# Two pipelined attention runs: a reordered head, with the first stack's issues dealt to two queues by halves

## Chip, cores and metric

The kernel runs on one core of one Trainium2 chip. The metric is the device time of one execution, in microseconds (us), the median of three runs.

## What is computed

The reference is a chain of four transformer layers on x of shape 8 x 256 x 128 (batch, tokens, features). Each has a modulation from a condition vector c, an attention and a feed-forward part:

```python
mod = (_silu(c) @ wmod).reshape(8, 6, 1, -1)          # sa, ca, ga, sb, cb, gb
ga = (2 * (ga >= 0) - 1) * jnp.maximum(jnp.abs(ga), 0.25)   # gb in the same way
h = _layernorm(x) * (1 + ca) + sa
x = x + ga * attention(h)
h = _layernorm(x) * (1 + cb) + sb
x = x + gb * feed_forward(h)
```

The change touches layer 0 (its attention with ALiBi slopes, and its feed-forward part, which is itself a rotary attention followed by a mixture of four experts) and the attention of layer 2. All three are causal, with 16 heads of 8 features. Shift, scale and gate of the feed-forward part are sb, cb and gb.

## The kernel before

**Runs and passes.** One pass m handles one batch of 256 tokens. The first pipelined run holds passes 0 to 15 (0 to 7 are the attention of layer 0, 8 to 15 its feed-forward part), the second one passes 16 to 23 (attention of layer 2). Each engine has its own program, in an order written out by hand; they meet only in semaphores. `pass_done` at the end of a phase opens the next one.

**Stacks.** Queries and keys (128 x 512 float32) are split into three bfloat16 parts each by GpSimd (`split_qk`, five instructions, lines 776 to 780). Small DMAs then copy them into a stack of rows that one matmul takes in full precision: `expand_half(queue, m, u)` issues 12 of them (6 for each side i of the partitions, which are partitions 0 to 63 and 64 to 127) for the half u of the heads, 24 a stack. There are three stacks, used in turn. Except for the first stack of a run, the Sync queue issues all 24. In pass 0 and in pass 16 Sync issues half u=0 and ScalarE's queue half u=1. The stack of pass m+1 can only be built after `parts_split(m)`; that of pass m+3 only once the turned scores of pass m have been computed, and the split of pass m+2 overwrites the parts of pass m, so that it waits until the stack of pass m has landed.

**Iterations.** The iteration for pass m (line `for m, there in iterations(ph)`) goes through six units k. In each, TensorE computes the turned scores of pass m (lines 1100 to 1108) and the scores of pass m+1 (lines 1074 to 1082, into the banks called `scored`), VectorE reduces the latter to maxima (`max_piped`, line 2169), and ScalarE takes the exponential of the former (`exp_piped`, line 3180). The iteration before pass `first` has the scores of the first pass alone. GpSimd splits the maxima (`split_max`, lines 762 to 766), TensorE turns them, and ScalarE puts them into the stack with two DMAs (`place_max`, line 3191); the turned scores need them.

**The head of a run.** Ahead of the iterations lie three fronts (passes first, first+1 and first+2). Each is: normalise (VectorE, `norm_piped`, line 2126), statistics of the pass two further on (`stats_piped`), turn (TensorE, line 1166), features (ScalarE, `take_normed`, line 3208), projections (TensorE, lines 1173 and 1177), intake (VectorE, lines 2176 and 2177), split (GpSimd). Each engine takes these in the order of its program. In between lie:

- on ScalarE, the issue of half u=1 of the first stack, behind the features of the first pass and ahead of those of the second
- in the first run, clearing three stacks by copies from a staging area: stacks 0 and 2 by VectorE (lines 2238 and 2241), stack 1 by ScalarE (line 3249); Sync and ScalarE wait for all of them (`stacks_clear`) before they issue
- on VectorE, behind all three fronts, `gates_piped` of the attention (four instructions, lines 2139 to 2144, that read `scored`), and in the first run `mod_ffn`: shift and scale of the feed-forward part (lines 2150 and 2151), its gates (the same four lines again, from `scored` again) and six small instructions (lines 2154 to 2159)
- on TensorE, behind the three fronts of the first run, the matmuls for these (`spread_mod`, line 1039): two groups at once and the third when `scored` has been read
- on GpSimd, behind the three fronts, `prepare_piped` (four clears, line 789, each with two settings of small areas)

The first scores of the first run wait for `mod_taken` 6, which is the end of all of VectorE's `mod_ffn`; those of the second run wait for the attention's gates.

## Time and profile before

| | |
|---|---|
| median of three runs | 2599.92 us (2599.36 to 2601.29) |
| the profiled execution, its own time | 2596.48 us |
| its span in the trace | 2594.7 us |
| mean granted TensorE clock | 0.767 |
| first run: first front to first reduction of scores | 9.5 to 57.7 us |
| second run: last x of the phase before to first reduction of scores | 1762.4 to 1805.2 us |

The trace is of one execution, so its span is what a sum of its rows explains; 1.8 us lie around it. The two heads are stretches of some 45 us each in which every engine is mostly idle. An engine name with a q (SPq, ACTq) is that engine's instruction queue issuing DMAs. Times within the trace count from the start of the span. Clock 1.00 is TensorE's upper level (2.4 GHz), 0.50 its lower one (1.2 GHz).

### The profile page before, as it was taken

To read this page: it belongs to the slowest core of one execution; us is meant where nothing else is said; L and a number is where in the kernel's file an instruction comes from. 1 tells how busy PE (TensorE), PEld (TensorE's weight loads), DVE (VectorE), ACT (ScalarE), POOL (GpSimd) and SP (SyncE) were. 2 spreads that over 40 slices of the span, in tenths; PEclk is the share of its full clock that TensorE was granted. 3 is DMA by queue.
4 is the path that set the end of the run, shared out by engine and by line. 5 is a ranking of instruction groups with operands and counts; after the bars stand their busy time and mean duration, and the time that the engine had idled before them with its cause. 6 is when DMAs were issued, how large, how long until landed. Compare 5 with 4: busy or idle time off the path is not lost.

```text
span 2594.7 us, 44049 instructions
## 1 busy us (share of the span) xinstructions
PE 1990.5 (77%) x14690; PEld 1394.5 (54%) x14690; DVE 1673.0 (64%) x5279; ACT 1148.5 (44%) x3370; POOL 894.2 (34%) x1171
## 2 busy tenths in 40 slices
PE   3878888874377667665687999994875799999945
PEld 2545666661265556554584666662543466667632
DVE  5787443335778887888847666664755466666547
ACT  1443333427677677767411222220442255565610
POOL 3433121014457655764540000003410155555512
PEclk7987889875555555555558999995995799999967
DMA  3111001010000000000010000001111000000000
GB/s 116 43 42 42 19 15 35 2 78 23 13 13 7 11 9 14 7 7 1 1 46 1 1 0 0 0 0 39 48 33 62 11 1 1 1 1 1 1 1 17
DMA packets 57809, 49.61 MB, mean 19 GB/s; under 512 B 7048, under 2 KB 55912, under 8 KB 57064
## 3 DMA queue, kind: packets, MB, share of 16 engines
q1 hardware_dynamic: 54548, 45.53, 5.5%
q10 hardware_dynamic: 3040, 1.38, 0.3%
q8 instruction: 108, 1.77, 0.3%
q14 instruction: 113, 0.93, 0.1%
HBM read 19.78 MB, written 1.05 MB: 8 GB/s over the span
## 4 chain that ended last, share of the span: by engine, by line
PE 44%; DVE 28%; ACT 8%; issue 7%; SPq 5%; POOL 5%; ACTq 1%; DMA 0%; DVEq 0%; POOLq 0%
PE bank L1544 5%; PE bank L1536 5%; PE bank L1537 5%; SPq L566 4%; DVE weights L2524 4%; PE bank L1613 3%; PE bank L1266 3%; ACT rope_c L3334 3%; ACT rope_s L3334 3%; PE bank L1282 3%; PE bank L1650 3%; PE bank L1662 2%; DVE small L2562 2%; DVE feat_o L2574 2%; POOL big L717 1%
## 5 line engine op out<-in xcount | busy, mean ns | idle before, releaser
L1450 PE MATMUL bank<-V,probsT 128*128 128x9 f32 x1024 | 234.7, 362 | 79.5 <-ACT probsT L3345 79.5
L1450 PEld LDWEIGHTS bank<-V,probsT 128*128 128x128 f32 x1024 | 224.9, 327 | 116.5 <-ACT probsT L3345 97.3
L2169 DVE TENSOR_REDUCE nmax<-bank 128x4 f32<-128x1024 f32 x144 | 176.1, 1223 | 81.3 <-PE bank L1082 81.2
L3400 ACT ACTIVATE hid<-bank 128x512 f32<-128x512 f32 x144 | 85.7, 597 | 283.3 <-PE bank L1537 272.0
L1544 PEld LDWEIGHTS bank<-weights,hid 128*128 128x128 f32 x1152 | 151.0, 192 | 78.9 <-issue 75.6
L2758 DVE TENSOR_TENSOR hid<-hid,bank 128x512 f32<-128x512 f32 x144 | 98.7, 688 | 127.3 <-PE bank L1544 123.2
L1544 PE MATMUL bank<-weights,hid 128*128 128x128 f32 x1152 | 152.5, 276 | 12.7 <-DVE hid L2758 10.3
L3345 ACT ACTIVATE probsT<-bank 128x512 f32<-128x512 f32 x128 | 76.0, 597 | 179.7 <-PE bank L1437 177.3
L1536 PE MATMUL bank<-O,weights 128*128 128x512 f32 x288 | 150.2, 604 | 2.7 <-DVE big L2698 2.7
L1537 PE MATMUL bank<-O,weights 128*128 128x512 f32 x288 | 148.3, 597 | 0.0
L804 POOL MEMSET big<- 128x4096 bf16 x1 | 3.5, 3511 | 411.7 <-DVE x L2796 411.7
L2772 DVE SCALAR_TENSOR_TENSOR O<-bank,O 128x128 f32<-128x128 f32 x496 | 138.9, 343 | 0.0
L2943 DVE TENSOR_TENSOR kT<-bank,weights 128x256 f32<-128x256 f32 x128 | 54.1, 423 | 123.3 <-PE bank L1613 123.1
L717 POOL TENSOR_TENSOR big<-big,rinv 128x512 f32<-128x512 f32 x128 | 131.7, 1050 | 4.0 <-DVE rinv L2936 4.0
L3434 ACT ACTIVATE big<-bank,nmax 128x256 f32<-128x256 f32 x256 | 118.7, 473 | 16.7 <-DVE nmax L2931 16.7
L3180 ACT ACTIVATE feat_o<-bank 128x1024 f32<-128x1024 f32 x72 | 73.7, 1024 | 117.5 <-PE bank L1108 87.9
L3180 ACT ACTIVATE O<-bank 128x1024 f32<-128x1024 f32 x72 | 73.8, 1024 | 110.2 <-PE bank L1108 82.4
L2451 DVE TENSOR_REDUCE nmax<-bank 128x2 f32<-128x512 f32 x128 | 84.9, 683 | 34.1 <-PE bank L1424 34.1
L1424 PE MATMUL bank<-qT 48*128 48x256 bf16 x256 | 70.3, 402 | 45.7 <-ACT weights L3288 33.3
L2931 DVE TENSOR_REDUCE nmax<-bank 128x2 f32<-128x512 f32 x128 | 82.3, 684 | 30.6 <-PE bank L1624 30.6
L725 POOL TENSOR_TENSOR kT<-kT 128x256 f32<-128x256 f32 x64 | 46.8, 731 | 137.4 <-DVE kT L2944 137.4
L1537 PEld LDWEIGHTS bank<-O,weights 128*128 128x128 f32 x288 | 55.5, 193 | 70.5 <-issue 70.5
(652 smaller groups left out, 5531.5 us busy)
## 6 DMA issues: line engine op xcount, KB each, us to landing
qT<-parts SPq DMA_DIRECT2D x276, 32.0 KB
big<-V SPq DMA_DIRECT2D x192, 32.0 KB
big<-parts SPq DMA_DIRECT2D x180, 32.0 KB
weights<-in_weights_l_ffn SPq DMA_DIRECT2D x1, 4832.0 KB, 15.0
weights<-in_weights_l_attn SPq DMA_DIRECT2D x1, 3904.0 KB, 12.7
weights<-in_weights_l_ffn SPq DMA_DIRECT2D x1, 3628.0 KB, 13.9
qT<-V SPq DMA_DIRECT2D x96, 32.0 KB
weights<-in_weights_l_ffn SPq DMA_DIRECT2D x1, 2304.0 KB, 7.8
```

The costliest lines, as they stand in the source:

```text
L566: queue.dma_start(stacks[m % STACKS][to, u * HALF:(u + 1) * HALF], pair_of(m, at, *of)).then_inc(stack_in[u].sem, 16)
L717: nc.gpsimd.tensor_tensor(row, row, rinv[:, h % H, :].unsqueeze(2).to_broadcast([P, T, S]), ALU.mult).then_inc(scaled.sem, 1)
L1450: last = mm(pb[1][:, t * S + h * wide:t * S + (h + 1) * wide], probsT[:, h % 2, at:at + P], values_of(b, k)[:, h * wide:(h + 1) * wide], s ...
L1536: mm(pb[two][:], W(ph, "gate")[:, cols], pair_feat, start=True, stop=True)
L1537: mm(pb[two + 1][:], W(ph, "up")[:, cols], pair_feat, start=True, stop=True).then_inc(hid_psum.sem, 1)
L1544: last = mm(pb[6 + e % 2][:, j * D:(j + 1) * D], risen(e)[:, j * P:(j + 1) * P], W(ph, "down")[:, e * D:(e + 1) * D], start=True, stop=True)
L2169: V_.tensor_reduce(to, scored.rearrange("p (i a n) -> p i a n", i=HPG, n=n), AX.X, ALU.max, negate=True).then_inc(score_max.sem, 1)
L2524: link(V_.tensor_scalar(at_most[:, j, :], row_of(b, j), tried[at][:, 0, j:j + 1], 0.0, ALU.is_le, ALU.add, accum_out=tried[at][:, 1, j:j + ...
L2772: last = V_.scalar_tensor_tensor(pair_sum[:, j, :], down[:, j, :], w, pair_sum[:, j, :], ALU.mult, ALU.add)
L3180: nc.scalar.activation(turned_probs[n % TURNS], turned_scores, ACT.Exp).then_inc(turned_exp.sem, 1)
L3334: nc.scalar.activation(signs[signed[0] % len(signs)], row_of(b, j), ACT.Sign, bias=tried[at][:, 0, j:j + 1], scale=-1.0, accum_out=tried[a ...
L3434: last = nc.scalar.activation(probs3[h % SLOTS3][:, t * S:(t + 1) * S], pb[h % 3][:, t * S:(t + 1) * S], ACT.Exp, bias=nmax[:, h % H, t:t ...
```

## The change

In ScalarE's program the features of the second pass now come ahead of its first issues, and those of the third pass in the middle of them. The first stack is dealt out by sides instead of by head halves: Sync issues side 0 of both halves, ScalarE side 1 of both, 12 DMAs each as before. In the first run ScalarE clears stacks 1 and 2, VectorE stack 0 alone. VectorE computes the attention's gates ahead of the intake of the second pass. TensorE computes the scale of the feed-forward part ahead of the third front, into `scored`, and VectorE takes it there ahead of the third intake; the feed-forward gates go through banks 4 and 5 (`raw`). The first scores wait for `mod_taken` 3 (mod, gates, scale), the first turned scores for 6.

```diff
@@ -557,9 +557,9 @@
             return 0 <= n < N3
-        def expand_half(queue, m, u):
-            for i in range(HPG):
+        def expand_half(queue, m, u, sides=range(HPG)):
+            for i in sides:
                 for slot, of in enumerate(SLOTS):
                     to = slice(64 * i + HD * slot, 64 * i + HD * slot + HD)
                     at = slice((2 * i + u) * HD * HALF, (2 * i + u + 1) * HD * HALF)
@@ -663,14 +663,14 @@
                         for i in range(HPG):
                             at = 64 * i + STACK_ROWS
                             sp.dma_start(stacks[m % STACKS][at:at + ALI_ROWS, :, 0, :], no_bias).then_inc(bias_gone, 16)
-                    for u in range(2 if m > first else 1):
+                    for u in range(2):
                         if m > first:
                             sp.wait_ge(stack_in[u].sem, stack_in[u](m, 0))
                         if m >= first + STACKS:
                             sp.wait_ge(turned_psum.sem, turned_psum(m - STACKS, 3 * u + 3))
-                        expand_half(sp, m, u)
+                        expand_half(sp, m, u, range(HPG) if m > first else (0,))
             load(1)
             for i, ph in enumerate(WEIGHED):
@@ -1039,13 +1039,16 @@
                     last = mm(to[:, b * D:(b + 1) * D], silu_n[:, b, :], W(ph, "wmod")[:, j * D:(j + 1) * D], start=True, stop=True)
                 last.then_inc(mod_psum, 1)
+            def scale_of_ffn(ph="l0_ffn"):
+                pe.wait_ge(loaded[1], 16)
+                pe.wait_ge(mod_taken, 2)
+                spread_mod(ph, 1, scored)
             def mod_ffn(ph="l0_ffn"):
-                pe.wait_ge(loaded[1], 16)
                 spread_mod(ph, 0, turned_scores)
-                spread_mod(ph, 1, ps[:, 4:6, :].rearrange("p c n -> p (c n)"))
-                pe.wait_ge(mod_taken, 2)
-                spread_mod(ph, 2, scored)
+                spread_mod(ph, 2, ps[:, 4:6, :].rearrange("p c n -> p (c n)"))
                 nc.tensor.transpose(pb[7][:, 0:P], W(ph, "n1"), C("ident"))
                 nc.tensor.transpose(pb[7][:, P:2 * P], W(ph, "n2"), C("ident"))
                 nc.tensor.transpose(pb[7][0:64, 2 * P:3 * P], W(ph, "lng"), C("ident"))
@@ -1055,7 +1058,7 @@
                 kind, u, h0 = UNITS[k]
                 if k == 0 and place_of(m) == 0:
-                    pe.wait_ge(mod_taken, 6 if m == 0 else MODS["l2_attn"] + 2)
+                    pe.wait_ge(mod_taken, 3 if m == 0 else MODS["l2_attn"] + 2)
                 if k == 0 and B <= m < B + STACKS:
                     pe.wait_ge(bias_gone, 16 * HPG * (m - B + 1))
@@ -1085,6 +1088,9 @@
             def turned_scores_piped(m, k):
                 kind, u, h0 = UNITS[k]
+                if k == 0 and m == 0:
+                    pe.wait_ge(mod_taken, 6)
                 if k % 3 == 0:
                     pe.wait_ge(nmax_in[u].sem, nmax_in[u](m + 1, 0))
@@ -1287,6 +1293,8 @@
                 first = RUNS[ph][0]
                 mod_piped(ph)
                 for m in fronts(ph):
+                    if m == 2:
+                        scale_of_ffn()
                     turn_normed(m)
                     project_qk(m)
                 if ph == "l0_attn":
@@ -2133,23 +2141,27 @@
                 link(V_.tensor_copy(shift_n, pb[6][:, 0:B]))
                 V_.tensor_scalar(scale_n, pb[6][:, B:2 * B], 1.0, None, ALU.add).then_inc(mod_taken, 1)
-            def gates_piped(to, n_psum, n_taken):
+            def gates_piped(to, n_psum, n_taken, raw):
                 dve.wait_ge(mod_psum, n_psum)
-                link(V_.tensor_scalar(mag_n, scored, -1.0, 0.25, ALU.mult, ALU.max))
-                link(V_.tensor_scalar(two_n, scored, 0.0, 2.0, ALU.is_ge, ALU.mult))
-                linkup()
-                link(V_.tensor_tensor(mag_n, scored, mag_n, ALU.max))
+                link(V_.tensor_scalar(mag_n, raw, -1.0, 0.25, ALU.mult, ALU.max))
+                link(V_.tensor_scalar(two_n, raw, 0.0, 2.0, ALU.is_ge, ALU.mult))
+                linkup()
+                link(V_.tensor_tensor(mag_n, raw, mag_n, ALU.max))
                 linkup()
                 V_.scalar_tensor_tensor(to, two_n, 1.0, mag_n, ALU.subtract, ALU.mult).then_inc(mod_taken, 1)
                 dve.wait_ge(mod_taken, n_taken)
+            def scale_of_ffn():
+                dve.wait_ge(mod_psum, 3)
+                V_.tensor_scalar(scale_ffn, scored, 1.0, None, ALU.add).then_inc(mod_taken, 1)
             def mod_ffn():
                 dve.wait_ge(mod_psum, 4)
                 V_.tensor_copy(shift_ffn, turned_scores).then_inc(mod_taken, 1)
-                V_.tensor_scalar(scale_ffn, ps[:, 4:6, :].rearrange("p c n -> p (c n)"), 1.0, None, ALU.add).then_inc(mod_taken, 1)
-                gates_piped(gates_ffn, 5, 5)
+                gates_piped(gates_ffn, 5, 5, ps[:, 4:6, :].rearrange("p c n -> p (c n)"))
                 dve.wait_ge(mod_psum, 6)
                 link(V_.tensor_copy(norm1_n, pb[7][:, 0:1]))
                 link(V_.tensor_copy(norm2_n, pb[7][:, P:P + 1]))
@@ -2230,16 +2242,21 @@
                 stats_piped(first)
                 mod_piped(ph)
                 stats_piped(first + 1)
-                for m in fronts(ph):
-                    norm_piped(m)
-                    stats_piped(m + 2)
-                    if m == 0:
-                        dve.wait_ge(ali_loaded, 16 * HPG * 2)
-                        V_.tensor_copy(stacks[0].rearrange("p g side n -> p (g side n)"), staging).then_inc(stacks_clear, 1)
-                    intake_piped(m)
-                    if m == 0:
-                        V_.tensor_copy(stacks[2].rearrange("p g side n -> p (g side n)"), staging).then_inc(stacks_clear, 1)
-                gates_piped(gates_attn, MODS[ph] + 2, MODS[ph] + 2)
+                norm_piped(first)
+                stats_piped(first + 2)
+                if ph == "l0_attn":
+                    dve.wait_ge(ali_loaded, 16 * HPG * 2)
+                    V_.tensor_copy(stacks[0].rearrange("p g side n -> p (g side n)"), staging).then_inc(stacks_clear, 1)
+                intake_piped(first)
+                norm_piped(first + 1)
+                stats_piped(first + 3)
+                gates_piped(gates_attn, MODS[ph] + 2, MODS[ph] + 2, scored)
+                intake_piped(first + 1)
+                norm_piped(first + 2)
+                stats_piped(first + 4)
+                if ph == "l0_attn":
+                    scale_of_ffn()
+                intake_piped(first + 2)
                 if ph == "l0_attn":
                     mod_ffn()
                 for m, there in iterations(ph):
@@ -3241,17 +3258,20 @@
             def piped(ph):
                 first = RUNS[ph][0]
-                for m in fronts(ph):
-                    take_normed(m)
-                    if m == first:
-                        if ph == "l0_attn":
-                            act.wait_ge(ali_loaded, 16 * HPG * 2)
-                            nc.scalar.activation(stacks[1].rearrange("p g side n -> p (g side n)"), staging, ACT.Copy).then_inc(stacks_clear, 1)
-                            act.wait_ge(stacks_clear, 4)
-                        else:
-                            act.wait_ge(ali_loaded, 16 * HPG * (2 + STACKS))
-                        act.wait_ge(parts_split.sem, parts_split(m, 1))
-                        expand_half(act, m, 1)
+                take_normed(first)
+                if ph == "l0_attn":
+                    act.wait_ge(ali_loaded, 16 * HPG * 2)
+                    for st in stacks[1:]:
+                        nc.scalar.activation(st.rearrange("p g side n -> p (g side n)"), staging, ACT.Copy).then_inc(stacks_clear, 1)
+                take_normed(first + 1)
+                if ph == "l0_attn":
+                    act.wait_ge(stacks_clear, 4)
+                else:
+                    act.wait_ge(ali_loaded, 16 * HPG * (2 + STACKS))
+                act.wait_ge(parts_split.sem, parts_split(first, 1))
+                expand_half(act, first, 0, (1,))
+                take_normed(first + 2)
+                expand_half(act, first, 1, (1,))
                 for m, there in iterations(ph):
                     for k in range(NU):
                         if m >= first and k == 2 and there(3):
```

## Rows read from the trace of the kernel before

**Rows 1.** Chain that ended last, from 1750 to 1970 us, its shares by line.
```profile
by line: SPq L566 52.7%; issue 9.3%; ACTq L566 3.9%; DVE big L1892 1.9%; PE bank L1544 1.7%; PE bank L1039 1.7%; DMA big<-V 1.4%; ACT O L3180 1.4%; DVE big L1873 1.4%; POOL big L979 1.3%; PE bank L1536 1.2%; PE bank L1537 1.2%; PE bank L117
```

**Rows 2.** Timeline, first head: start, length, engine, line, what, [idle before <- releaser].
```profile
11.14 3.78 PE L1039 MATMUL bank<-weights,feat_o 128*128 128x128 f32 x16
...
15.85 3.60 ACT L3249 ACTIVATE big<-big 128x4096 bf16<-128x4096 f32 x1
...
17.97 2.29 DVE L2241 CAST big<-big 128x4096 bf16<-128x4096 f32 x1
...
18.12 2.60 POOL L776 CAST parts<-weights 128x512 bf16<-128x512 f32 x1 [5.04 <-DVE weights L2177]
...
24.62 8.80 SPq L566 DMA_DIRECT2D qT<-parts  x12
24.62 9.79 ACTq L566 DMA_DIRECT2D qT<-parts  x12
...
34.46 0.56 ACT L3208 ACTIVATE V<-bank,small 128x256 f32<-128x256 f32 x1 [15.01 <-issue]
...
38.13 0.66 POOL L776 CAST V<-weights 128x512 bf16<-128x512 f32 x1 [12.84 <-DVE weights L2177]
...
39.65 0.56 ACT L3208 ACTIVATE V<-bank,small 128x256 f32<-128x256 f32 x1 [4.62 <-PE bank L1166]
```

**Rows 3.** Timeline, first head: modulation of the feed-forward part, first reduction.
```profile
42.14 4.24 PE L1039 MATMUL bank<-weights,feat_o 128*128 128x128 f32 x32
...
43.57 1.22 DVE L2139 TENSOR_SCALAR feat_o<-bank 128x1024 f32<-128x1024 f32 x1
...
48.62 2.55 PE L1039 MATMUL bank<-weights,feat_o 128*128 128x128 f32 x16 [2.24 <-DVE weights L2144]
...
57.69 1.23 DVE L2169 TENSOR_REDUCE nmax<-bank 128x4 f32<-128x1024 f32 x1 [1.08 <-PE bank L1082]
```

**Rows 4.** Timeline of the Sync queue: issues of whole stacks (24) or half ones (12).
```profile
42.63 17.64 SPq L566 DMA_DIRECT2D big<-V  x24
60.38 18.37 SPq L566 DMA_DIRECT2D big<-parts  x24
...
84.99 17.93 SPq L566 DMA_DIRECT2D qT<-V  x24
...
1781.02 8.78 SPq L566 DMA_DIRECT2D big<-parts  x12
...
1798.24 17.43 SPq L566 DMA_DIRECT2D big<-V  x24
...
1905.59 18.33 SPq L566 DMA_DIRECT2D big<-V  x24
```

**Rows 5.** Timeline, second head and the first iterations behind it.
```profile
1778.05 0.34 DVE L2012 TENSOR_SCALAR small<-small 128x2 f32<-128x2 f32 x1
...
1790.07 0.56 ACT L3208 ACTIVATE V<-bank,small 128x256 f32<-128x256 f32 x1 [16.71 <-issue]
...
1804.63 0.52 POOL L789 MEMSET big<- 128x512 f32 x1
...
1805.24 1.23 DVE L2169 TENSOR_REDUCE nmax<-bank 128x4 f32<-128x1024 f32 x1 [1.15 <-PE bank L1082]
...
1811.35 0.20 POOL L762 CAST small<-nmax 128x16 bf16<-128x16 f32 x1 [4.02 <-DVE nmax L2169]
...
1819.65 1.02 ACT L3180 ACTIVATE feat_o<-bank 128x1024 f32<-128x1024 f32 x1 [3.17 <-PE bank L1108]
...
1832.14 0.61 POOL L780 CAST V<-weights 128x512 bf16<-128x512 f32 x1
```

**Rows 6.** Stretches: bounds, length, busy time of each engine, granted clock, DMA share, GB/s.
```profile
22.00:26.00 4.00, 0.69 (x2) 0.29 (x2) 1.77 (x7) 0.00 (x0) 3.06 (x4) 0.50 0.00 0
...
314.00:330.00 16.00, 16.00 (x99) 13.69 (x98) 2.81 (x12) 5.38 (x14) 0.00 (x0) 1.00 0.01 3
```

**Rows 7.** Chain that ended last in order of time: landing of the last stack.
```profile
1922.38 3.19 DMA big<-V
```

## Prediction, made before the change was run

> **What bounds the kernel now.** I read the stretches and the chain that ended last first, since busy shares say nothing of two short heads. In the second run, that chain goes through the Sync queue for more than half of the stretch around it [rows 1]: behind the first stack, which the two queues issue by halves, six stacks lie between the issue at 1798.24 and the last one at 1905.59, 107.35 us or 17.9 us a stack, where 24 issues of 0.73 us take 17.5 [rows 4]. Sync goes from one stack into the next without a rest. So this run ends as many us earlier as the stack of its second pass is begun earlier, unless another engine then falls behind. In the first run the queue has one rest: the stack of pass 2 is issued by 60.38 + 18.37 = 78.75, that of pass 3 starts at 84.99 [rows 4]. It waits for the split of pass 3, which hangs on the iterations; these hang on the first reduction of scores at 57.69 [rows 3]. The rest is 6.2 us.
>
> What holds both heads up is plain in the timeline. ScalarE issues 12 DMAs from 24.62 to 34.41 and only then takes the features of pass 1 at 34.46 [rows 2]; in the second run that row is 1790.07 [rows 5]. VectorE, TensorE and GpSimd stand still meanwhile.
>
> **First run: Sync queue.** ScalarE now clears two stacks: 15.85 + 3.60 + 3.60 = 23.05 [rows 2]. The split of pass 0 takes 4.50 us where nothing is in its way (start of pass 1's split 38.13, issue behind it 42.63) [rows 2, 4]; its first instruction took 2.60 us instead of 0.66 beside VectorE's copy of 17.97, which goes away [rows 2]. So it ends at 22.6, and the issues start at 23.05 instead of 24.62. Sync's 12 take 8.80 and end at 31.9.
>
> The Trainium skill (SBUF — State Buffer, section Who interferes with whom) says that VectorE in a two-port mode and GpSimd lock each other out for a whole instruction. The trace agrees: 2.60 for 0.66 beside the copy [rows 2]. If the split kept its 2.60 without the copy, Sync's first issue would slip to 24.6, which the 6.2 us of rest absorb: the sum stays.
>
> Features of pass 1: ScalarE at 23.0. From that row to the split it took 38.13 - 34.46 = 3.67 [rows 2]; TensorE's clock was low then and is low between 22 and 26 [rows 6], so I keep it: split 26.7 to 31.2. The new gates ahead of the intake cost 48.62 - 43.57 = 5.05 [rows 3]; they start when the statistics are done, about 2.0 us behind the intake of pass 0 (18.0 + 2.0; the same two steps end at 1778.39, and the split there began at 1781.02 - 4.50 = 1776.5 [rows 4, 5]). They end at 25.1, while the intake needs the projections of about 25.8: hidden, with 0.7 to spare. The stack of pass 1 starts at 31.9 instead of 42.63: 10.7 earlier. That of pass 2 follows by 31.9 + 17.64 + 18.37 + 0.1 = 68.1.
>
> **First run: VectorE, which the first reduction hangs on.** ScalarE's six issues (half of 9.79, 4.9) run from 23.6 to 28.5. TensorE goes from the projections, 25.8, into the eight groups for the scale, which wait for the feed-forward weights too; no DMA moves between 22 and 26 [rows 6], so these have landed. They take 2.55 [rows 3] to 3.78 us [rows 2]; with 3.4 they end at 29.2. Turn and features of pass 2 follow as in the trace (from 38.1, where the intake hands over to the split, to the end of the copy at 39.65 + 0.56) [rows 2]; of these 2.1 us I take 1.4 for what lies from TensorE's turn on: features to 30.6. Projections to 32.2, between 1.3 and 2.1 us of them. Scale on VectorE, 1.22 as its neighbour [rows 3], is done at 30.4, before the intake at 32.2, hidden. Two groups of modulation: 4.24, as they took right behind the projections of pass 2 before [rows 3], to 36.5 (at the low clock twice 3.78, to 39.8). Shift on VectorE is hidden under the second. Gates 5.05, to 41.6; the six small instructions 0.4 (51.17 + 5.05 = 56.2, and VectorE's idle time starts at 57.69 - 1.08 = 56.6) [rows 3]. The scores of unit 0 no longer wait for them, so the reduction follows at 42.0; I take 42.4, since the scale's groups may run lower still. Before, it was 57.69 [rows 3]: 15.3 earlier. Removed are on VectorE's path one stretch of ScalarE's issues (9.8), the third spread that waited on `scored`, the scores' own 1.1, and gates that now run while VectorE had idled.
>
> GpSimd: the second six issues of ScalarE end at 30.6 + 4.9 = 35.5 and land by 37.2, with 1.7 us from the end of an issue (1905.59 + 18.33 = 1923.9) to its landing (1922.38 + 3.19 = 1925.6) [rows 4, 7]. The split of pass 2 waits for that, runs to 41.7, and its clears, four of 0.52 us with two settings each, about 2.8 together [rows 5], to 44.5. GpSimd is needed at 42.4 + 6.1 = 48.5 (1811.35 - 1805.24) [rows 5]: hidden, 4.0 to spare.
>
> Does Sync follow? Its rest of 6.2 allows 10.7 + 6.2 = 16.9; 15.3 is less. The stack of pass 3 starts at 84.99 - 15.3 = 69.7, behind 68.1. All later waits of the run are between things that move together: **15.3 us**. Bounds: 12.0 (all modulation matmuls at the low clock, 39.8 instead of 36.5) and 16.9 (the rest of the queue).
>
> **Second run.** Gates start at 1778.4 and end at 1783.4. The features of pass 17 are taken at about 1778.0 and its projections ready at 1780.9, so here the gates do delay the intake, by 2.5. Intake 1784.3, split to 1788.8. Sync's first 12 end at 1781.02 + 8.78 = 1789.8 [rows 4]: the split comes 1.0 before, so the gates cost nothing. The stack of pass 17 starts at 1789.9 instead of 1798.24: **8.35 us**. If the gates ran 2 us long it would be 7.3.
>
> Behind the gates wait intake, normalisation of pass 18 (1785.2), its features (1786.5, 0.9 behind the end of ScalarE's first six at 1785.5), ScalarE's second six (to 1791.1, landed 1792.8), and GpSimd's split of pass 18, which needs the landing: to 1797.3, clears to 1800.1. TensorE has the first scores at 1789.8, VectorE reduces at 1790.0 instead of 1805.24 [rows 5], and would have its third maximum at 1796.1. GpSimd's split of the maxima now waits 4.0 us behind its own clears, and TensorE, in order, holds units 4 and 5 behind it. Against the first exponential at 1819.65, which came 8.3 behind the split of the maxima [rows 5], I get 1800.1 + 8.3 - 0.5 = 1807.9 (less 0.5, as unit 4 no longer waits for unit 3's maximum), 11.7 earlier instead of 15.2. The split of pass 19 then ends at 1832.75 - 11.7 = 1821.1 [rows 5], and Sync comes to it at 1789.9 + 2 x 17.5 = 1824.9. The new wait has 3.8 to spare, so the run stays with the queue and 8.35 stands. Bounds: 6.0 and 10.5, from the 2.2 by which its six stacks exceed 6 x 17.53.
>
> **Sum.** 15.3 + 8.35 = 23.6. The profiled execution would come to 2596.48 - 23.6 = 2572.8; it is 3.4 under the median of the runs, 2599.92, so the median would be **2576.3**. Bounds of the terms: 18.0 to 27.4, or 2572.5 to 2581.9.
>
> **Rivals.**
> - The queue leads the first run. If the stack of pass 3 were ready as soon as Sync is, or if the iterations turned out to lean on stacks 1 and 2, the first run gains 10.7: 19.0 in all, 2580.9. For it: 17.5 us a stack against iterations of 15.5. Against: the rest before 84.99. Chance 0.12.
> - GpSimd becomes the new wait of the second head. It has 3.8 to spare; with ScalarE's second half later by 6 us, for instance, 2.2 of the 8.35 are lost: 2578.5. Chance 0.06.
> - The change doesn't do what it says: something behind both heads absorbs the time, 2599.9. The chain of rows 1 speaks against it. Chance 0.04.
> - Slower, through TensorE's clock. The feed-forward stretch 314 to 330 is TensorE busy throughout at the upper level [rows 6]; at the lower one it takes 16 us more. The head sets when TensorE's dense stretches begin. If in two of the eight feed-forward passes such a stretch ran low, that costs 32 against 23.6 won: 2608. It decides from 1.5 passes on. Against: the work ahead of these stretches stays as it is. Chance 0.04.
> - Forecast: 0.74.
>
> Three runs agree within 0.1%, and about 0.2%, 5.2 us, can be told from no change. Faster by more than that are the forecast and the first two rivals, 0.92; within it 0.04; slower 0.04. The range takes the bounds of the terms and 4 to 6 us on either side for single matmul groups at the other clock (1.2 us a group of 8, 3.78 against 2.55): 2568 to 2588.
>
> **What the profile would show.** Features of pass 1 at about 23 with the queue's issues behind them in two blocks of six; Sync's whole stacks from 32 and from 1789.9; the first reductions at 42.4 and 1790; stack of pass 3 from 69.7 and behind 68.1; the second run's stacks still end to end; GpSimd's first split of maxima at 1800.1 behind its clears. The prediction fails if the reduction at 42.4 comes while the stack of pass 3 doesn't follow it, if VectorE's gates end after the projections in the first head, or if the granted clock in the feed-forward passes falls.

## Result and the profile after

The changed kernel takes 2573.52 us in the median of four runs (2569.91 to 2575.62), against 2599.85: a ratio of 0.9895, 95% interval 0.9881 to 0.9909, so 24 to 31 us faster. Forecast were 2576.3, within 2568 to 2588. The profiled execution has a span of 2570.2 us, 24.5 less than before, where the sum said 23.6. The median came out 2.8 under the forecast mostly because the sum was put on top of the 3.4 us by which the profiled execution before lay under its median; in the changed kernel that distance is 1.5.

The Sync queue's timeline of the changed kernel answers to [rows 4] (start, length, queue, what):

```profile
23.03 8.86 SPq L566 DMA_DIRECT2D qT<-parts  x12
32.00 17.82 SPq L566 DMA_DIRECT2D big<-V  x24
49.92 18.38 SPq L566 DMA_DIRECT2D big<-parts  x24
69.01 17.93 SPq L566 DMA_DIRECT2D qT<-V  x24
...
1744.53 0.33 SPq L619 DMA_DIRECT2D weights<-in_weights_l_ffn  x1
...
1763.19 8.78 SPq L566 DMA_DIRECT2D big<-parts  x12
1772.08 17.71 SPq L566 DMA_DIRECT2D big<-V  x24
1789.89 17.43 SPq L566 DMA_DIRECT2D qT<-parts  x24
1807.44 17.92 SPq L566 DMA_DIRECT2D big<-V  x24
...
1879.41 18.06 SPq L566 DMA_DIRECT2D big<-V  x24
```

In the first run, the stack of pass 1 starts at 32.00 (31.9 was worked out), that of pass 3 at 69.01 (69.7), 15.98 earlier than before, with 49.92 + 18.38 = 68.30 ahead of it (68.1). In the second run times count best from the start of its phase, which is the weights' issue at 1744.53 here and at 1762.37 before: the stack of pass 17 starts 27.55 behind it instead of 35.87, 8.32 earlier (8.35). The six stacks behind it still lie end to end, and the chain that ended last, over the stretch of [rows 1] moved by 18 us (1732 to 1952), is Sync's issues by 56.5%, where it was 52.7:

```profile
by line: SPq L566 56.5%; issue 9.8%; PE bank L1021 3.0%; POOL big L979 2.6%; PE bank L1015 1.9%; PE bank L1552 1.7%; PE bank L1039 1.7%; DVE big L1881 1.4%; ACT O L3197 1.4%; PE bank L1544 1.2%; PE bank L1545 1.2%; DMA big<-V 1.1%; PE bank
```

The first head's timeline, beside [rows 2, 3]:

```profile
15.90 7.11 ACT L3265 ACTIVATE big<-big 128x4096 bf16<-128x4096 f32 x2
...
18.16 0.66 POOL L776 CAST parts<-weights 128x512 bf16<-128x512 f32 x1 [4.91 <-DVE weights L2189]
...
22.91 0.55 ACT L3225 ACTIVATE V<-bank,small 128x256 f32<-128x256 f32 x1
...
25.38 3.52 PE L1039 MATMUL bank<-weights,feat_o 128*128 128x128 f32 x16
25.69 0.48 DVE L2188 TENSOR_SCALAR weights<-bank,weights 128x256 f32<-128x256 f32 x1 [0.84 <-PE bank L1183]
...
29.17 4.53 ACTq L566 DMA_DIRECT2D qT<-parts  x6
...
30.75 3.73 PE L1039 MATMUL bank<-weights,feat_o 128*128 128x128 f32 x32
...
37.38 0.61 POOL L776 CAST parts<-weights 128x512 bf16<-128x512 f32 x1 [5.49 <-DMA qT<-parts]
...
38.17 2.14 DVE L2152 SCALAR_TENSOR_TENSOR weights<-O,feat_o 128x1024 f32<-128x1024 f32 x1
...
40.76 1.15 DVE L2181 TENSOR_REDUCE nmax<-bank 128x4 f32<-128x1024 f32 x1
```

Features of pass 1 are taken at 22.91 instead of 34.46, the first cast of GpSimd's split is down to 0.66, and VectorE reaches its first reduction at 40.76 instead of 57.69, with no wait for TensorE ahead of it (a wait would stand in brackets behind the row).

The second head, beside [rows 5]:

```profile
1760.46 1.21 DVE L2147 TENSOR_SCALAR feat_o<-bank 128x1024 f32<-128x1024 f32 x1
...
1767.86 0.56 ACT L3225 ACTIVATE V<-bank,small 128x256 f32<-128x256 f32 x1 [7.14 <-PE bank L1172]
1767.87 4.43 ACTq L566 DMA_DIRECT2D big<-parts  x6
...
1770.17 0.61 POOL L780 CAST V<-weights 128x512 bf16<-128x512 f32 x1
...
1771.98 1.23 DVE L2181 TENSOR_REDUCE nmax<-bank 128x4 f32<-128x1024 f32 x1 [0.22 <-PE bank L1085]
...
1776.83 0.61 POOL L776 CAST parts<-weights 128x512 bf16<-128x512 f32 x1 [5.28 <-DMA big<-V]
...
1783.95 0.20 POOL L762 CAST small<-nmax 128x16 bf16<-128x16 f32 x1
...
1791.57 1.02 ACT L3197 ACTIVATE feat_o<-bank 128x1024 f32<-128x1024 f32 x1 [2.45 <-PE bank L1114]
```

The split of pass 17 is over at 1770.78, 1.2 ahead of Sync's end at 1771.97 (1.0 was worked out). GpSimd's split of pass 18 waits for both halves of the first stack to land (the bracket names the tile of the next stack, whose DMAs count on the same semaphores), and only behind it and the clears come the maxima at 1783.95: the new wait that was foreseen.

What became of the head's gain shows in the stretches between three weight loads on Sync, each of which follows the end of a phase: the first run but for the tail of its last expert passes, that tail, and the second run. Lengths in us, from the profiled execution of each kernel; their experiments follow:

| kernel | first run | its tail | second run | ratio of times (95%) |
|---|---|---|---|---|
| before | 443.04 | 121.33 | 189.36 | |
| changed | 427.34 | 119.09 | 181.38 | 0.9895 (0.9881 to 0.9909) |
| changed, once more | 427.02 | 117.66 | 181.49 | 0.9917 (0.9895 to 0.9939) |
| first head alone | 427.40 | 119.09 | 188.92 | 0.9929 (0.9916 to 0.9941) |
| second head alone | 443.02 | 117.57 | 181.88 | 0.9964 (0.9950 to 0.9977) |
| issues alone | 433.71 | 116.77 | 179.60 | 0.9912 (0.9898 to 0.9926) |
| modulation alone | 439.39 | 121.65 | 191.61 | 0.9984 (0.9975 to 0.9993) |
| by halves | 424.48 | 117.65 | 188.43 | 0.9941 (0.9919 to 0.9962) |
| clears as before | 433.86 | 121.54 | 180.83 | 0.9924 (0.9900 to 0.9947) |
| ScalarE shares the second stack | 424.81 | 121.30 | 178.14 | 0.9903 (0.9879 to 0.9926) |
| the same, clears early | 427.30 | 121.74 | 178.94 | 0.9887 (0.9864 to 0.9910) |
| other tile | 426.60 | 117.64 | 181.92 | 0.9904 (one run each) |
| other order of slots | 428.73 | 121.75 | 181.52 | 0.9930 (one run each) |
| six shared, other tile, clears early | 428.41 | 121.74 | 177.88 | 0.9887 (0.9865 to 0.9908) |

The first run gives 15.7, the second 7.98. The tail's 2.24 is not the change's: with the second head alone changed, nothing differs up to there, and it is 3.76 shorter than before. All that lies outside the three stretches is 1.4 us longer than before, and so the span's gain is 24.5 and not the 23.7 of the two runs. The stretch of the tail before (bounds, length, busy time of each engine, granted clock, DMA share, GB/s), and in the kernel with the second head alone:

```profile
443.04:564.37 121.33, 106.93 (x892) 79.79 (x890) 32.55 (x110) 40.21 (x81) 4.13 (x13) 0.87 0.02 7
```

```profile
443.02:560.59 117.57, 101.94 (x883) 77.35 (x882) 31.82 (x108) 40.14 (x81) 4.13 (x13) 0.91 0.02 7
```

The granted clock is 0.87 in one and 0.91 in the other, and TensorE is busy 5 us less. In these expert passes TensorE is busy for 87 to 88% of the stretch, and they come out 4 us apart in kernels that do the same there. Later sessions had the kernel before at 2594.7 to 2596.5 in the median, 3 to 5 us lower than the first; so ratios of one session compare best, and smaller differences are read from the stretches. These have a spread too. The second run takes 180.8 to 181.9 us in the six kernels that have the changed order there, but the first run takes 424.8 to 428.7 in the eight that have the changed first head; a difference under 4 us in the first run shows only in the rows of its head.

### The profile page after: what moved, and what is told of

It is laid out like the page before. It is cut to its first block, busy times and chain, and to the rows that moved or that the text cites. A ratio compares the mean times of both kernels' runs of the same rounds, so it can differ in the third digit from the quotient of the medians.

```text
span 2570.2 us, 44049 instructions
## 1 busy us (share of the span) xinstructions
PE 1990.2 (77%) x14690; PEld 1397.4 (54%) x14690; DVE 1668.7 (65%) x5278; ACT 1152.4 (45%) x3371; POOL 893.2 (35%) x1171
## 3 DMA queue, kind: packets, MB, share of 16 engines
HBM read 19.78 MB, written 1.05 MB: 8 GB/s over the span
## 4 chain that ended last, share of the span: by engine, by line
PE 44%; DVE 27%; issue 8%; ACT 8%; SPq 7%; POOL 5%; ACTq 1%; DMA 0%; DVEq 0%; POOLq 0%
SPq L566 6%; PE bank L1552 5%; PE bank L1544 5%; PE bank L1545 5%; DVE weights L2541 4%; PE bank L1621 3%; ACT rope_c L3354 3%; ACT rope_s L3354 3%; PE bank L1658 3%; PE bank L1272 2%; PE bank L1670 2%; PE bank L1288 2%; DVE small L2579 2%; DVE feat_o L2591 2%; POOL big L717 1%
## 5 line engine op out<-in xcount | busy, mean ns | idle before, releaser
L1552 PE MATMUL bank<-weights,hid 128*128 128x128 f32 x1152 | 152.5, 276 | 12.8 <-DVE hid L2775 10.4
## 6 DMA issues: line engine op xcount, KB each, us to landing
weights<-in_weights_l_ffn SPq DMA_DIRECT2D x1, 4832.0 KB, 15.3
```

The source lines that it names most:

```text
L1552: last = mm(pb[6 + e % 2][:, j * D:(j + 1) * D], risen(e)[:, j * P:(j + 1) * P], W(ph, "down")[:, e * D:(e + 1) * D], start=True, stop=True)
```

## Experiments

### One head at a time

Two kernels; the first has the change in the first run only, the second in the second run only (in ScalarE's, Sync's and VectorE's programs):

```diff
+                if ph == "l0_attn":      # or "l2_attn"
                     ... the changed order
+                else:
+                    ... the order before
```

> The first head as changed, the second as before. My theory: the first run gains what its first reduction of scores gains (57.69 to 40.76 in the changed kernel, and 15.98 at the stack of pass 3), so 16 to 18 us under the kernel before, about 2583, with the Sync queue's stack of pass 3 at 69.0 and the second run's stack of pass 17 15 to 18 us after where the changed kernel has it plus 8. Rival, the Sync queue leads the first run: 10.6 us, 2589.

> The second head as changed, the first as before. My theory: the run is led by the Sync queue, so it gains the 8.3 us by which the stack of pass 17 starts earlier, about 2591.8; the stacks of the run stay end to end. Rival, the iterations lead it: their start gains about 11.4 to 13 us, 2587 to 2588.5. Rival, GpSimd's late split of maxima takes part of it: 5 us or less, 2595.

Measured: 2578.68 us, 0.9929 of the kernel before in the same session (median 2595.19), and 2586.31 us, 0.9964. As shares of the time, 0.71% and 0.36% add up to 1.07%, and the whole change is 1.05%. In the traces the first head brings 15.64 in its own run, and the stack of pass 3 starts at 69.08. The second brings 7.5; its stack of pass 17 starts 27.54 behind the start of the phase, 8.33 earlier than before. The rival of 10.6 us for the first run is out: it lies outside the interval of 15 to 22 us, and the stretch says 15.6. That the queue leads was this rival's reason, and it is half true: in this kernel the stack of pass 3 begins 0.13 us behind the end of the one before it (50.61 + 18.34 = 68.95), so the queue's rest is used up. In the second run, a lead of the iterations would have had to show as 11 us or more; the stretch shows less.

### Issues alone, modulation alone

The first has ScalarE's order, clears and sides of the change, the second VectorE's and TensorE's modulation and gates:

```diff
 issues alone, against the changed kernel:
-                gates_piped(gates_attn, ..., scored)     # ahead of the second intake
-                    scale_of_ffn()                       # ahead of the third
+                gates and mod_ffn behind the third intake, through scored, as before
 modulation alone, against the changed kernel:
-                take_normed(first + 1)                   # ahead of the issues
-                expand_half(act, first, 0, (1,))
-                take_normed(first + 2)
-                expand_half(act, first, 1, (1,))
+                expand_half(act, first, 1)
+                take_normed(first + 1), take_normed(first + 2)
```

> Features, clears and dealing by sides as changed in both heads; the gates and the feed-forward modulation stay in their old places and banks. My theory: in the first head VectorE has intake 2 at 32.1, then gates to 37.1, shift and scale to 39.6, the second gates to 44.7, small ones and scores to a first reduction at 46.2, 11.5 earlier than before, while the Sync queue could gain 16.8. The second head keeps its 8 us, since the gates then end at the same time as GpSimd's clears. Sum 19.5 us, 2580.4. Rival, the queue leads the first run: as fast as the changed kernel, 2574 to 2576. Rival, the modulation is what matters: within 10 us of the kernel before.

> Gates and feed-forward modulation as changed (places and banks); issues, features and clears as before. My theory: the features of pass 1 still wait for 12 issues, to 34.4, so the first reduction is at 53.4, 4.3 us earlier, and the second run gains nothing, since its stack of pass 17 starts where it did. 2595.6. Together with the run that has only the issues this adds up to the whole change. Rival, the modulation alone is worth 9 us or more: 2591 or less. Rival, nothing without the other part: 2599.9.

With the issues alone the time was 2573.43 us, 0.9912: 19 to 27 us. The timeline of VectorE in that kernel (start, length, line, what):

```profile
32.04 0.48 DVE L2176 TENSOR_SCALAR weights<-bank,weights 128x256 f32<-128x256 f32 x1 [3.37 <-PE bank L1177]
...
32.83 1.22 DVE L2139 TENSOR_SCALAR feat_o<-bank 128x1024 f32<-128x1024 f32 x1
...
43.64 1.23 DVE L2144 SCALAR_TENSOR_TENSOR weights<-O,feat_o 128x1024 f32<-128x1024 f32 x1
...
46.47 1.22 DVE L2169 TENSOR_REDUCE nmax<-bank 128x4 f32<-128x1024 f32 x1 [1.08 <-PE bank L1082]
```

From 32.83 to 45.4 VectorE works without a pause at gates, shift, scale, gates and small ones, and the reduction follows at 46.47 (46.2 was expected). The stack of pass 3 started at 74.59, 10.4 earlier than before, though Sync had been free since 50.86 + 18.49 = 69.35: in this kernel VectorE leads the first run up to there, not the queue. In the changed kernel the two are all but level. In the trace shown above Sync rests 0.6 us before the stack of pass 3. When the same kernel ran once more, it did not rest at all, and neither did it in the six other kernels that have this first head (0.11 to 0.13 us lie between the two stacks, as between any two that are issued end to end). The rows of the second trace:

```profile
51.78 18.25 SPq L566 DMA_DIRECT2D big<-parts  x24
70.15 17.93 SPq L566 DMA_DIRECT2D qT<-V  x24
```

The rest of 6.2 us is thus spent: a first reduction that came still earlier would bring at most 0.6 us more at the stack of pass 3. The second run's 179.60 is as short as with the whole change, so the gates' new place brings nothing there. The whole gain is 3 us above the expected one; the tail, 4.6 us shorter than before, is more than that, and the first run gained 9.3 us where 11.5 were expected.

With the modulation alone it was 2592.28 us, 0.9984: 2 to 6 us, with 4.3 expected. The features of pass 1 came at 35.68, behind 12 issues from 25.84 on, the first reduction at 52.10, and the stack of pass 3 at 80.62, 4.37 earlier. 0.88% and 0.16% add up to 1.04%: as shares of the time the two parts add, and so they do at the first reduction (11.22 and 5.59, against 16.93). Most of the gain is that of the issues, clears and sides together; the rest comes only through VectorE's list, in the first run. The modulation's second run did not stay as it was: it took 191.61 us, 2.2 more than before, although its stack of pass 17 starts 35.94 behind the start of the phase (35.87 before). Of these, 1.7 lie behind the last stack, at a granted clock of 0.84 where it was 0.93; what lowered it stays open.

### The first stack by halves again

The title of this document speaks of halves; the change deals the first stack by sides, and it is the kernel before that dealt it by halves of the heads. This kernel goes back to that and keeps the rest of the change.

```diff
-                expand_half(act, first, 0, (1,))
+                expand_half(act, first, 1, (0,))
                 take_normed(first + 2)
                 expand_half(act, first, 1, (1,))
```

Sync issues half 0, both sides, accordingly.

> The changed kernel, but the first stack is dealt by halves of the heads again (Sync half 0, ScalarE half 1), with the features of pass 2 still in the middle of ScalarE's issues. My theory: dealing by sides is worth nothing in the first run (VectorE is busy with gates until 40.8 and the half would land by 33.6) and nothing in the second (half 0 lands at 1773.6 instead of 1770.9, the first reduction moves by 2.7, but GpSimd's clears hold the split of the maxima to 1783.9 anyway, and the Sync queue leads): 2573 to 2575 as the changed kernel. Rival, the early half counts: 2 to 3 us slower than the changed kernel.

Measured: 2581.09 us, 0.9941. This expectation failed, and so did the rival's size. The Sync queue's timeline of this kernel's second head has:

```profile
1759.16 8.78 SPq L566 DMA_DIRECT2D big<-parts  x12
1774.34 17.43 SPq L566 DMA_DIRECT2D big<-V  x24
```

The stack of pass 17 starts 15.18 behind that of pass 16, where by sides it was 8.89. The waits of the Sync queue have the reason:

```profile
SPq L669 <- DMA big<-parts: 6.3, 1, 6.3
SPq L669 <- DMA qT<-parts: 2.1, 1, 2.1
```

Sync waits for half 0 of the first stack to land before it issues half 0 of the next one, 6.3 us in the second head and 2.1 in the first. Dealt by sides, half 0 had been issued some 4.4 us earlier (half of 8.78) by both queues together, and had landed by the time that Sync got there: the changed kernel has no such wait. The kernel before had it, in both heads (the waits of its Sync queue, that of the second head first; the wait in total, how often, the longest):

```profile
SPq L669 <- DMA big<-parts: 6.1, 1, 6.1
SPq L669 <- DMA qT<-parts: 2.8, 1, 2.8
```

There Sync's 12 issues ended at 1789.80, half 0 had landed 6.1 later, at 1795.9, and the late split of pass 17 held Sync for the last 2.2 us only, to 1798.24 [rows 4]. So two waits ended close to each other, and the late features were only the second: without them the stack of pass 17 comes 2.0 us earlier in this kernel (33.83 behind the start of the phase, 35.87 before), and dealing by sides brings the other 6.3 (27.55). The second run took 188.43 us, against 181.38 changed and 189.36 before: by halves, 7 of the 8 us are gone.

In the first head the wait is 2.1 us. It is not quite covered there: the first reduction came at 39.47, 1.3 earlier than in the changed kernel, but the stack of pass 3 at 70.39, 1.4 later, right behind the end of the stack before it (52.03 + 18.24 = 70.27). The run took 424.48 all the same, within the spread of the first run given above; its last stretch, from 350 us on, ran at a granted clock of 0.98 where the changed kernel had 0.93.

### The clears as before

```diff
-                    for st in stacks[1:]:
+                    for st in stacks[1:2]:
```

and VectorE copies stack 2 behind the intake of pass 0 again.

> The changed kernel, but VectorE clears stack 2 again behind the intake of pass 0, ScalarE stack 1 alone. My theory: VectorE's gates move by 2.3, to 27.4, and now hold up the intake of pass 1 by 1.7; GpSimd's first cast takes 2.6 again, so the queues begin at 24.6; the first reduction and the stack of pass 3 come 1.6 to 2 us later: 2575.5. Rival, no part of it is on the path: as the changed kernel.

Measured: 2579.41 us, 0.9924. The changed kernel did not run beside it, and the intervals of the two ratios overlap (0.9900 to 0.9947 here, 0.9881 to 0.9909 there); so its trace decides. VectorE and GpSimd in that kernel:

```profile
19.46 2.28 DVE L2252 CAST big<-big 128x4096 bf16<-128x4096 f32 x1
19.61 2.60 POOL L776 CAST parts<-weights 128x512 bf16<-128x512 f32 x1 [6.09 <-DVE weights L2189]
21.66 1.86 DVE L2134 TENSOR_SCALAR xb<-x,small 128x128 f32<-128x128 f32 x2
...
24.36 1.01 DVE L2020 TENSOR_SCALAR small<-small 128x2 f32<-128x2 f32 x1
25.29 1.21 DVE L2147 TENSOR_SCALAR feat_o<-bank 128x1024 f32<-128x1024 f32 x1
```

The gates start at 25.29 instead of 19.99. Of these 5.3 us, 2.3 are the copy; 1.0 and 0.7 are VectorE's two normalisations (1.86 instead of 0.89) and a small one (1.01 instead of 0.34) that stretch beside GpSimd's casts; the rest lies ahead of the copy, where this run was slower (the intake of pass 0 at 18.67 instead of 17.22). The first reduction came at 45.80 instead of 40.76 and the stack of pass 3 at 73.05 instead of 69.01. The Trainium skill (SBUF — State Buffer, section Who interferes with whom) has a rule for such pairs, an exclusive lock between VectorE in a two-port mode and GpSimd; the stretched rows on both sides agree with it (2.60 for 0.66, 1.86 for 0.89).

The direction was right and the size too small: 1.6 to 2 expected, 5 at the first reduction and 4 at the stack of pass 3, of which up to 1.5 is that run's slower start. Moving the clear off VectorE, which looks like housekeeping, is worth 2.5 to 4 us of the first head. The whole first run was 6.5 us longer (433.86); what comes on top of the head's 4 is within the spread of that stretch.

### Is the second run led by the queue?

ScalarE takes over half 1 of the second run's second stack, which Sync leaves out; and in a further kernel GpSimd's clears also come ahead of its third split:

```diff
                 expand_half(act, first, 1, (1,))
+                if ph == "l2_attn":
+                    act.wait_ge(parts_split.sem, parts_split(first + 1, 1))
+                    act.wait_ge(stack_in[1].sem, stack_in[1](first + 1, 0))
+                    expand_half(act, first + 1, 1)
 and on GpSimd
+                    if m == first + 2:
+                        prepare_piped(ph)
                     split_qk(m)
```

> The changed kernel, and in the second run ScalarE also issues half 1 of the stack of pass 17 (12 DMAs behind its own second six, 1774 to 1783, ahead of the first split of maxima). My theory: the queue leads, so Sync begins the stack of pass 18 at 1782.6 instead of 1789.9, but then waits for the split of pass 19 at 1804.6 instead of 1807.4, and gains 2.7 us on the changed kernel: 2571. Rival, a wait of the iterations already limits the run: nothing gained. Rival, half the issues saved count in full: 7 us, 2566.5.

> As the run before, and GpSimd's clears come ahead of its split of the third pass, in the time in which it waits for the landing of the first stack (1771.6 to 1776.8). My theory: the split of the maxima comes 2.6 us earlier, so do the split of pass 19 and with it the stack of pass 19 (1802.0 instead of 1807.4): 5.4 us under the changed kernel, 2568. This also tells what GpSimd's wait in the second head costs once the queue doesn't cover it. Rival, the clears are off the path: the same as the run before.

Measured: 2570.88 us, 0.9903, and 2567.69 us, 0.9887. The stack of pass 19 starts 60.27 behind the start of the phase with the sharing, 59.82 with the clears early as well, and 62.91 in the changed kernel. So the first expectation, 2.7, met with 2.64, and the run is 3.2 shorter. Sync begins the stack of pass 18 6.0 us earlier and then waits: with its issues relieved the queue gains only until the iterations hold it, after 2.64 us, where the prediction had worked out a slack of 3.8. The second expectation, 5.4, met with 3.1 at the stack of pass 19, and the run itself was no shorter than with the sharing alone (178.94, 178.14). What took the place of GpSimd's clears is in ScalarE's timeline of that kernel:

```profile
1779.53 8.94 ACTq L566 DMA_DIRECT2D big<-V  x12
1788.51 0.37 ACT L3205 ACTIVATE probsT<-bank 24x256 bf16<-24x256 f32 x1 [17.40 <-DMA big<-V]
```

and in GpSimd's:

```profile
1784.09 0.20 POOL L762 CAST small<-nmax 128x16 bf16<-128x16 f32 x1
```

GpSimd splits the maxima at 1784.09, but ScalarE is still issuing till 1788.47 and places them then. That is 41.28 behind the start of the phase, where the changed kernel has 41.22: the split gained 2.6 us and the place nothing. The 12 added issues had become the wait.

### Why the first stack lands late

In the changed kernel's second head GpSimd's split of pass 18, which waits for the first stack to land, starts 4.5 us behind ScalarE's last issue (1767.87 + 4.43 = 1772.30, split at 1776.83), where I had 1.7. Two experiments, on the tile and on the order of the slots:

```diff
 tile:
-            stacks[m % STACKS]
+            stacks[(m if m < 2 * B else m - 2 * B) % STACKS]
 order:
-                for slot, of in enumerate(SLOTS):
+                for slot, of in (list(enumerate(SLOTS)) if not ScalarE's queue else list(enumerate(SLOTS))[::-1]):
```

> The changed kernel, but the second run's passes take the three stacks in another order, so that its first stack lies in qT as that of the first run does, and no longer in big. To see: how long behind the last issue the first stack lands. In the changed kernel the split of pass 18, which waits for it, starts 4.5 us behind ScalarE's last issue, at a DMA share of 0.6; in the first head 3.7 us behind, at a share of 0.3. Theory: the tile decides, the share falls to 0.3 and the split starts 3.7 us or less behind. Rival: something else of the second head decides, and share and landing stay. The Sync queue leads either way, so the time stays within 1 us of the changed kernel's.

> The changed kernel, but ScalarE issues the six slots of each side in reverse order, so that the two queues never write the same slot rows at once. If it is queues in step with each other that slow the landing in the second head, the DMA share there falls from 0.6 towards 0.3 and the first stack lands 1 us or more earlier. Rival: the order is nothing to it, share 0.6 and a split of pass 18 at 4.5 us behind the last issue as before. The time stays within 1 us of the changed kernel's either way.

The times, 2569.91 and 2576.59 in one run each, tell nothing at this spread. The stretches do (columns as above). Of the changed kernel, while ScalarE issues its second six and behind them, and last the like place of the first head:

```profile
1767.00:1769.00 2.00, 1.22 (x3) 0.79 (x4) 1.10 (x7) 0.56 (x1) 1.82 (x3) 0.50 0.45 79
...
1771.00:1773.00 2.00, 0.92 (x12) 0.27 (x12) 1.78 (x3) 0.00 (x0) 0.55 (x1) 0.50 0.65 74
1773.00:1775.00 2.00, 0.96 (x12) 0.32 (x12) 0.93 (x2) 0.00 (x0) 0.00 (x0) 0.50 0.61 75
...
29.00:31.00 2.00, 1.34 (x9) 1.12 (x8) 1.17 (x1) 0.56 (x1) 1.86 (x3) 1.00 0.29 81
```

Of the kernel with the other tile, whose head begins 2.2 us earlier (issues from 1761.01 instead of 1763.19):

```profile
1766.00:1768.00 2.00, 1.70 (x4) 1.17 (x4) 0.04 (x1) 0.24 (x1) 1.79 (x4) 0.50 0.28 83
...
1769.00:1771.00 2.00, 0.56 (x12) 0.23 (x12) 1.71 (x3) 0.00 (x0) 0.37 (x1) 0.50 0.52 82
1771.00:1773.00 2.00, 0.73 (x12) 0.19 (x8) 1.22 (x1) 0.00 (x0) 0.00 (x0) 0.50 0.34 60
```

Of the kernel with the other order, whose head begins 4.1 us later:

```profile
1775.00:1777.00 2.00, 0.95 (x12) 0.31 (x12) 1.81 (x3) 0.00 (x0) 0.61 (x1) 0.50 0.64 74
```

With the order turned round nothing changes: 0.64 for 0.65, and the split of pass 18 starts at 1780.90, again 4.5 behind the last issue (1771.93 + 4.43 = 1776.36). With the other tile the share falls early in the head to the first head's 0.28, then rises to 0.52 where it was 0.65, and is at 0.34 in the next stretch, where it was 0.61; GpSimd's split starts 3.8 behind the last issue (1765.69 + 4.46 = 1770.15, split at 1773.96), 0.7 sooner, as much as in the first head (29.17 + 4.53 = 33.70, split at 37.38: 3.7). So the tiles that the stacks go to decide 0.7 us of the 2.8 by which I was wrong, in the direction that its theory said, and short of what it expected in the share. One run each is thin, but other traces bear it out. With the first stack in big, the split starts 4.5 to 4.7 behind the last issue in five of them (the changed kernel twice, the other order, both kernels with the sharing); in the last experiment, which has it in qT as well, it starts 3.5 behind (1771.72 + 4.49 = 1776.21, split at 1779.67), and the share stays between 0.26 and 0.31 from 1770.9 to 1778.9. Why even the first head's tile takes 3.7 where the last stack of the second run took 1.7 [rows 4, 7] stays open; that stack comes from one queue, this one from two at once, but no experiment here tells just this apart.

### Six instead of twelve

The last experiment puts these together, in the second run: six of the second stack's DMAs on ScalarE, the other tile, the clears early. Against the kernel with twelve, the line that deals them out:

```diff
+                    expand_half(act, first + 1, 1, (1,))
```

> In the second run ScalarE issues six DMAs of the stack of pass 17 (side 1 of half 1) instead of twelve, the stacks are taken in the order that puts the first into qT, and GpSimd's clears come ahead of its third split. With twelve, ScalarE's issues ran into the first place of the maxima by 3.4 us. My theory: Sync begins the stack of pass 18 at 39.5 to 40.5 behind the start of the phase (45.4 in the changed kernel) and that of pass 19 at 58.7 (62.9), with the split of the maxima and ScalarE no longer in the way: 4 us under the changed kernel, 1 under the run with twelve. Rival: the iterations lead from pass 19 on and nothing is won over the run with twelve.

> The changed kernel once more, beside the others, since its own runs spread over 5.7 us: 2570 to 2576.

Measured: 2568.53 us, 0.9887, beside 2575.01, 0.9917, for the changed kernel once more. The stack of pass 18 starts 40.70 behind the start of the phase (39.5 to 40.5 expected) and that of pass 19 58.24 (58.7 expected), with GpSimd's split of the maxima at 1784.16 and ScalarE's place of them at 1785.96. The second run takes 177.88 us, 3.6 less than the changed kernel's 181.49 of the same session; the intervals of the two ratios, 0.9865 to 0.9908 and 0.9895 to 0.9939, still touch. It has the fastest second run of all that were tried, 1.1 us under the kernel with twelve. Sync has no rest left between the stacks of passes 18 and 19 (1789.10 + 17.43 = 1806.53, next at 1806.64), so ScalarE's issues no longer hold it. As three things differ at once, the shares of each are not shown.

## Why the prediction was right

**First run, Sync queue.** Every step held: issues from 23.03 (23.05), stack of pass 1 at 32.00 (31.9), features at 22.91 (23.0), the split's cast at 0.66 once the copy was gone. The gates ahead of the intake were hidden under the projections, by 0.84 us in the row of 25.69 (0.7).

**First run, VectorE.** The reduction came at 40.76, not 42.4. TensorE was better than taken: the projections of pass 2 and two groups ran at the upper clock (1.00 in the stretch 29 to 31; 3.73 us for the two, 4.24 taken), and the shift was over before the gates. One term was missed and lost 0.9: VectorE's last gate instruction took 2.14 instead of 1.22 beside GpSimd's split. The gain at the stack of pass 3 is 15.98 against 15.3, within the bounds of 12.0 and 16.9. It is less than the 16.93 at the reduction: six maxima and the first exponential (55.08, 17.0 earlier) still had it, and the rest went in the iteration behind. It could hardly have been more: the bound of 16.9 was the queue's rest, and 0.6 us or nothing of it was left.

**Second run.** 8.32 at the stack of pass 17 against 8.35, 7.98 at the end. The kernel with the second head alone shows the same. But what I named as its cause, the late features, was only 2.0 to 2.2 us of it. The sum has Sync go from its 12 issues straight into the stack of pass 17 once the split is done, and never priced its wait for half 0 to land. That wait was 6.1 us in the kernel before, hidden in time behind the split, and is 6.3 by halves. Dealing by sides took it away, which I had not reasoned; so that the term came out to 0.03 us is in this part luck. The landing of a first stack was mis-sized, 1.7 against 4.5 (and 3.7 in the first head). GpSimd's split of the maxima came 1.7 later than worked out for it, and the first exponential 1.5 later (1791.57, where 1807.9 less the 17.8 of this run's earlier start is 1790.1); the slack, 3.8 by my sum and 2.6 as measured by sharing the issues, took it.

**Rivals.** The rival of a queue that leads the first run and holds its gain at 10.7 is out: the gain is 15.6 to 15.7, and with the issues alone Sync is idle from 69.35 to 74.59. With the whole change the queue does catch up with it. GpSimd's wait is real but covered, and worth 0.4 us at the stack of pass 19 where it was taken away. Nothing behind the heads absorbed the time. The expert passes did move, by 2.2 us in favour in the profiled execution and by 5 us across kernels (116.8 to 121.7), far from the 32 of the slower rival. With the 1.4 us lost elsewhere they leave 0.8 of the 24.5 us that the heads did not bring.

## What to carry to other kernels

Work out for each run of a pipeline which list leads it, the queue's issues or an engine's instructions, and what rest the other has: a head is worth what it gives to the leading one, up to that rest. Here VectorE's list led the first run until the queue's rest was used up, and the queue led the second. When a step is found late, list every wait of the engine that it holds, with the time at which each ends: behind the late split lay a landing that ended only 2.2 us before it, and the same 24 issues, dealt by sides instead of by halves, made 7 of 8 us in the second run. And where an engine is given more issues to do, its next instruction that others wait for must fit behind them.

## What was not expected of the hardware

A DMA's landing behind its issue is no constant. 24 DMAs of 32 KB went out from two queues in both heads, in 9.1 us in the second (1763.19 to 1772.30) and in 10.7 in the first (23.03 to 33.70, with ScalarE's features between its two sixes). In the second the DMA share came to 0.6, and the work that waits for the last of them began 4.5 us behind the last issue; in the first it stood at 0.3 and that time was 3.7. By halves, Sync's own 12 had landed 6.3 and 2.1 us behind their last issue. The Trainium skill (DMA: Bandwidth & Descriptors, section Issuing engines are not separate DMA queues) says that issuing from several engines saves only the time to issue, which is usually small beside the DMA itself. The first half agrees: two queues issue a stack in 9 us instead of 17.5. The second does not hold here, where 24 issues of 0.73 us set the pace of a whole run, and the landing behind the last issue was longer with two queues (3.7 and 4.5 us against the 1.7 of one stack from one queue). The expert passes take 116.8 to 121.7 us in kernels that have the same instructions in them. TensorE's busy time goes with it (100.9 in the shortest, 106.9 in the kernel before), and its mean granted clock only roughly: 0.90 in the longest, 0.91 in one of 117.7.
